# Two transformer layers on one core: the score matmuls of a step in another order, and one bias addition on another engine

## The chip, the cores and the metric

The kernel runs on one core of a Trainium2 chip. A core has a matrix engine (TensorE, "PE" in the profile, with its weight loads shown as "PEld"), a vector engine (VectorE, "DVE"), a scalar engine (ScalarE, "ACT"), a general engine (GpSimd, "POOL") and an engine that mostly starts transfers (SyncE, "SP"). Each runs its own list of instructions in order, and they meet at semaphores. Matmuls write to eight PSUM banks of 128 partitions by 512 fp32 values; VectorE and ScalarE read them.

The metric is the device time of one execution in microseconds. Three executions took 332.4, 333.36 and 334.31 us, so the median before is 333.36 us.

## The reference

Two layers run one after the other over eight batches of 256 tokens of width 128. Each layer is attention with 16 heads of size 8 and a feed-forward part, each followed by a residual sum and a layer norm:

```python
x = L0_attn_x
x = _layernorm(x + _L0_attn_ref(x, ...), axis=-1)     # 16 heads, softmax over 256 keys
x = _layernorm(x + _L0_ffn_ref(x, ...), axis=-1)      # 128 -> 512, butterfly, gelu, butterfly, 512 -> 128
x = _layernorm(x + _L1_attn_ref(x, ...), axis=-1)     # low-rank q and kv, rope, causal softmax
x = _layernorm(x + _L1_ffn_ref(x, ...), axis=-1)      # silu(gate) * up, dequantised weights
```

The attention of layer 0 and the first half of its feed-forward part are

```python
scores = jnp.einsum('bqhd,bkhd->bhqk', q, k) * scale
attn = jax.nn.softmax(scores, axis=-1)
out = jnp.einsum('bhqk,bkhd->bqhd', attn, v)
...
h = jnp.einsum('bsd,dh->bsh', x, W_exp) + b_exp
h = butterfly(h, up_weights, D_HIDDEN)
h = jax.nn.gelu(h + up_bias, approximate=False)
```

The kernel folds `W_exp` and the butterfly into one 128x512 matrix `wup` and one bias `bhid`, so that the way up of layer 0 is a matmul, a bias per row and a gelu.

## The kernel before

**Heads and steps.** Both layers' batches make one list of 16 batches, so 256 heads in all. The program of every engine is one loop, `for g in STEPS`, in steps of four heads (`QUAD`). The softmax needs the maximum of each row of scores before the exponential, so every head's scores are computed twice: first with queries on the partitions, for the maximum ("max" scores, `max_scores`, line 388), and 12 heads later (`LEAD`) with keys on the partitions, for the exponential ("exp" scores, `exp_scores`, line 398). A third matmul subtracts the maximum in PSUM (`less_maximum`, line 407 in layer 0, line 411 in layer 1). VectorE takes the maxima out of the banks (line 824 in layer 0, lines 830 to 832 in layer 1), TensorE turns eight heads' maxima at a time (`turn_maxima`, line 465), ScalarE copies them to `mt` (line 672), and ScalarE applies Exp to each head's bank (line 728).

**Strips.** A head has eight features, and a matmul of its scores uses 32 of the array's 128 rows. Head m stands in strip m mod 4. So heads g, g+1 are in strips 0 and 1, and heads g+2, g+3 in strips 2 and 3; the maxima of step g are for heads g+12 to g+15, in the same order of strips.

**The two halves of a step on TensorE.** Step g first runs `scores((g+14, g+15), (g, g+1), at)` and then `scores((g+12, g+13), (g+2, g+3), at + 4)`. Each call waits for its four banks, and for the keys and the turned maxima that it needs, all at its head; then it issues the two halves of the two maxima and of the two exp scores in turns, so that all four strips have work, and ends with two `less_maximum`.

**Banks.** The eight banks change roles from step to step: the first half of step g uses banks at to at+3, the second half banks at+4 to at+7. After its scores a step runs other work (projections, transposes, products with V, the feed-forward parts), each in a bank claimed from at to at+3 (`claim`). The second half of the next step takes the banks at to at+3 of the step before: its maxima the first two, its exp scores the last two. So it waits until the other work's banks have been read. Layer 0's claims go to banks 0, 2, 3, 1 in order of claim, layer 1's to 2, 3, 0, 1, and those of the step after the gelu's to 0, 1, 2, 3.

**The way up of layer 0.** Two batches make a tile of 512 tokens; there are four tiles. Tile n's four chunks (line 546) run two in step 32n+52 and two in step 32n+56. VectorE reads each chunk's bank, adds the bias and writes `hid0` (line 893, "room_a" in the profile). It does so after the four maxima of its step, and ahead of the residual sum `r_a` (line 915), of the statistics (lines 793 and 796) and of the next step's maxima. ScalarE applies Gelu to all of `hid0` in step 32n+60 (line 763), with a table load before and after it.

## Time and profile before

| | us |
|---|---|
| median of three executions | 333.36 |
| the profiled execution | 331.46 |
| its span (first to last instruction) | 329.7 |
| TensorE busy | 281.9 (85%) |
| VectorE busy | 263.6 (80%) |
| ScalarE busy | 207.4 (63%) |
| GpSimd busy | 205.6 (62%) |

The profiled execution took 331.46 us, 1.76 us more than its span. The span is what the rows further down divide up. "Busy" leaves out waits, branches and the start of transfers. A busy matrix engine is not an engine at its peak, since matmuls overlap and their ends are modelled. In groups of instructions, the name on the left of the arrow is the tile that is written, and the part behind the last bar is the time in which the engine stood idle just before these instructions, with what ended it.

### The profile page before, as it was taken

What the parts mean: (1) busy time and instruction counts of PE and PEld (TensorE: products, weight loads), DVE (VectorE), ACT (ScalarE), POOL (GpSimd) and SP (SyncE); (2) the same over time, 40 slices, a digit from 0 to 9 for tenths busy, and PEclk for the clock granted to TensorE, in tenths of its full rate; (3) what the DMA queues carried; (4) which work ended last, traced back from release to release, by engine and by line L of the source; (5) the groups of instructions that cost most, each with busy time, mean ns of one, the idle gap of its engine ahead of it and who ended that gap; (6) DMA issues with size and microseconds to landing.
All of it is one profiled execution on the core that took longest, in us unless ns stands there. A gap on an engine that the chain in (4) does not pass through costs nothing.

```text
span 329.7 us, 9464 instructions
## 1 busy us (share of the span) xinstructions
PE 281.9 (85%) x3194; PEld 199.3 (60%) x3194; DVE 263.6 (80%) x1007; ACT 207.4 (63%) x428; POOL 205.6 (62%) x326
## 2 busy tenths in 40 slices
PE   7989989997989989888997887988898888898763
PEld 3667555654666446554675456766676666666553
DVE  4897887879588888899679697687899999965565
ACT  2576865776857668496986569666385757536110
POOL 0549994471348447583779785697769756457332
PEclk9999969999899999999999799997799999899978
DMA  6684250303030220404022130403114040000000
GB/s 229 251 248 158 81 195 3 129 0 129 3 112 18 61 101 18 145 8 139 18 64 99 33 130 6 136 23 99 65 27 153 1 146 4 19 2 17 18 16 32
DMA packets 20495, 25.84 MB, mean 78 GB/s; under 512 B 3744, under 2 KB 14304, under 8 KB 20320
## 3 DMA queue, kind: packets, MB, share of 16 engines
q1 hardware_dynamic: 20016, 24.72, 22.4%
q8 instruction: 26, 0.43, 0.6%
q10 hardware_dynamic: 432, 0.53, 0.5%
q14 instruction: 21, 0.17, 0.2%
HBM read 6.36 MB, written 1.05 MB: 22 GB/s over the span
## 4 chain that ended last, share of the span: by engine, by line
PE 42%; DVE 32%; issue 12%; ACT 7%; POOL 4%; DMA 1%; POOLq 0%; ACTq 0%; DVEq 0%
PE bank L600 13%; DVE mx L824 7%; DVE room_c L832 6%; PE bank L615 4%; PE bank L398 4%; PE bank L388 4%; ACT E L728 3%; PE bank L465 3%; DVE turned L923 2%; PE bank L482 2%; DVE room_a L893 2%; DVE room_c L858 2%; PE bank L556 2%; PE bank L567 2%; DVE mx L832 2%
## 5 line engine op out<-in xcount | busy, mean ns | idle before, releaser
L728 ACT ACTIVATE E<-bank 128x512 f32<-128x512 f32 (+1 forms) x256 | 120.3, 550 | 78.4 <-PE bank L411 41.5
L824 DVE TENSOR_REDUCE mx<-bank 128x2 f32<-128x512 f32 x128 | 78.9, 679 | 9.3 <-PE bank L388 9.2
L832 DVE CUSTOM_DVE_ANT_0 room_c<-bank,mask_sb 128x256 f32<-128x256 f32 (+1 forms) x256 | 72.7, 349 | 1.3 <-PE bank L388 1.1
L398 PE MATMUL bank<-QK 32*128 32x256 f32 x480 | 55.8, 316 | 18.5 <-DVE hid L860 6.8
L388 PE MATMUL bank<-QK 32*128 32x256 f32 x480 | 56.8, 313 | 8.1 <-DVE mx L832 2.6
L600 PE MATMUL bank<-E,V 128*32 128x256 f32 (+1 forms) x1024 | 60.7, 383 | 0.1
L398 PEld LDWEIGHTS bank<-QK 32*128 32x128 f32 x480 | 36.9, 188 | 29.3 <-issue 21.8
L388 PEld LDWEIGHTS bank<-QK 32*128 32x128 f32 x480 | 37.2, 187 | 23.3 <-issue 8.9
L1052 POOL TENSOR_SCALAR_AFFINE_SELECT E<-E 128x512 f32<-128x512 f32 x64 | 39.2, 638 | 11.4 <-ACT E L728 11.3
L600 PEld LDWEIGHTS bank<-E,V 128*32 128x32 f32 x1024 | 31.5, 117 | 23.5 <-issue 7.0
L923 DVE STREAM_TRANSPOSE turned<-bank 128x256 f32<-128x256 f32 x32 | 14.3, 446 | 21.8 <-PE bank L600 21.8
L1059 POOL TENSOR_TENSOR at<-turned,rec 128x256 f32<-128x256 f32 x16 | 10.1, 632 | 28.0 <-DVE rec L945 28.0
L407 PE MATMUL bank<-mt,const_r 32*128 32x512 f32 x128 | 27.6, 419 | 0.0
L1032 POOL TENSOR_TENSOR parts<-qk,parts 128x512 f32<-128x512 f32 x15 | 19.2, 1278 | 13.3 <-ACT parts L698 13.3
L556 PE MATMUL bank<-xt,wf 128*128 128x256 f32 x96 | 25.6, 410 | 1.3 <-ACT E L728 0.9
L411 PE MATMUL bank<-mt,const_r 32*128 32x256 f32 (+1 forms) x256 | 24.5, 275 | 0.0
L990 POOL TENSOR_SCALAR nm_a<-mv_a 128x2 f32<-128x2 f32 x15 | 2.9, 193 | 33.1 <-DVE mv_a L796 33.1
L556 PEld LDWEIGHTS bank<-xt,wf 128*128 128x128 f32 x96 | 18.4, 202 | 4.8 <-ACT E L728 1.5
L832 DVE DVE_READ_ACCUMULATOR2_ANT mx<- 128x1 f32 x256 | 21.2, 83 | 0.0
L411 PEld LDWEIGHTS bank<-mt,const_r 32*128 32x128 f32 x256 | 19.2, 189 | 0.0
L465 PE MATMUL bank<-const_r,mxp 128*128 128x128 f32 x64 | 14.8, 314 | 4.6 <-DVE mx L824 3.5
L735 ACT ACTIVATE QK<-spread_qk 128x1024 fp32r<-128x1024 f32 x16 | 17.2, 1076 | 0.0
(127 smaller groups left out, 558.7 us busy)
## 6 DMA issues: line engine op xcount, KB each, us to landing
spread_qk<-parts SPq DMA_DIRECT2D x30, 256.0 KB, 2.5
spread_qk<-parts SPq DMA_DIRECT2D x60, 128.0 KB, 2.1
room_c<-room_c SPq DMA_DIRECT2D x64, 32.0 KB, 1.9
xb<-x_nat SPq DMA_DIRECT2D x1, 1024.0 KB, 6.9
out<-ln_g SPq DMA_DIRECT2D x7, 128.0 KB, 1.9
xt<-x_t SPq DMA_DIRECT2D x1, 768.0 KB, 6.7
wi<-wi_all SPq DMA_DIRECT2D x1, 576.0 KB, 4.4
room_c<-fac_u SPq DMA_DIRECT2D x1, 508.0 KB, 6.5
```

Of the source, the lines that this page charges most:

```text
L388: ins = nc.tensor.matmul(g_bank["max", m][:, cols], both[:, 0, c * P:(c + 1) * P], both[:, 1, keys], start=True, stop=True)
L398: nc.tensor.matmul(g_bank["exp", m][:, c * T:(c + 1) * T - q0], both[:, 1, c * P:(c + 1) * P], both[:, 0, q0:T], start=(c == 0), stop=False)
L407: ins = nc.tensor.matmul(g_bank["exp", m][:, :].rearrange("p (c t) -> p c t", c=2), ones, most.unsqueeze(1).broadcast_to([STRIP, 2, T]), s ...
L411: ins = nc.tensor.matmul(g_bank["exp", m][:, c * T:(c + 1) * T - c * P], ones, most[:, c * P:T], start=False, stop=(c == 1))
L465: ins = nc.tensor.matmul(bank[:, q * P:(q + 1) * P], mxp[:, n % 2, q, :], const_r[:, 0, :], start=True, stop=True)
L556: ins = nc.tensor.matmul(bank[:, s * T:(s + 1) * T], wf[:, s, c * P:(c + 1) * P], xt[:, i * T:(i + 1) * T], start=True, stop=True)
L600: ins = nc.tensor.matmul(bank[VCOL * j:VCOL * (j + 1), q0:T], values, E[:, (2 * n + e) % E_RING, j, k * T:(k + 1) * T - q0], start=(e == 0 ...
L728: act.activation(E[:, a % E_RING, j, 0:n], g_bank["exp", m][:, 0:n], ACT.Exp, scale=SCALE)\
L824: ins = nc.vector.tensor_reduce(mx[:, n % 2, :, i], bank[:, :].rearrange("p (q k) -> p q k", q=QT), AX.X, ALU.max, negate=True)
L832: ins = nc.vector.tensor_tensor_reduce(out=masked_s[:, at % 2, lo:hi], in0=bank[:, lo:hi], in1=mask_sb[:, T + lo - hi:T], scale=-1.0, scal ...
L923: nc.vector.transpose(turned[:, t, :], g_bank["pv", n][:, 0:T]).then_inc(A["turned"], 1)
L1052: nc.gpsimd.affine_select(out=e, in_=e, pattern=[[0, 4], [1, P]], compare_op=ALU.is_ge, fill=0.0, base=0, channel_multiplier=-1).then_inc( ...
```

## The change

There are two parts.

**The order of the scores.** The function `scores` is split up. In a step, the maxima of heads g+14, g+15 and the exp scores of heads g, g+1 still go in turns, and wait for their four banks first. The wait for the turned maxima (`mt_ready`, in every second step) now stands behind these scores, right ahead of `less_maximum`. Then the exp scores of heads g+2, g+3 wait for their own two banks only, run without maxima between them, and are followed by their `less_maximum`. Then the maxima of heads g+12, g+13 wait for their two banks and run last.

**The bias of the way up.** The read of the chunk's bank with the bias goes from VectorE's list to ScalarE's: an `Identity` with `bias=bhid[:, c:c + 1]`, behind the step's four Exps, its copies of maxima, projection and transposed tokens, and ahead of `high_parts`, `copy_values` and the Gelu.

```diff
-            def scores(maxima, exps, at):
-                for i, m in enumerate(maxima):
-                    take((at + i) % BANKS, ("max", m), A["max_done"], order_of(m))
-                for i, m in enumerate(exps):
-                    take((at + len(maxima) + i) % BANKS, ("exp", m), A["exp_done"], m + 1)
...
+            def step_scores(g, at):
+                ahead = range(g + LEAD, g + LEAD + QUAD)
+                banks_for_maxima(ahead[2:], at)
+                banks_for_exps((g, g + 1), at + 2)
                 for long in range(2):
-                    for m in exps if first else ():
+                    for m in ahead[2:]:
+                        max_scores(m, 1 - long)
+                    for m in (g, g + 1):
                         exp_scores(m, long)
-                    for m in maxima:
-                        max_scores(m, 1 - long)
-                    for m in () if first else exps:
+                if g % 8 == 0:
+                    pe.wait_ge(A["mt_ready"], g // 8 + 1)
+                for m in (g, g + 1):
+                    less_maximum(m)
+                banks_for_exps((g + 2, g + 3), at + QUAD + 2)
+                for c in range(2):
+                    for m in (g + 2, g + 3):
+                        exp_scores(m, c)
+                for m in (g + 2, g + 3):
+                    less_maximum(m)
+                banks_for_maxima(ahead[:2], at + QUAD)
+                for c in (1, 0):
+                    for m in ahead[:2]:
+                        max_scores(m, c)
...
         @block.scalar
...
+                for c in range(HC):
+                    if (n := tile_at(g, AT_UP0[c])) is not None:
...
+                        act.wait_ge(F0["up_ps"], HC * n + c + 1)
+                        act.activation(hid0[:, c, :], g_bank["up0", n, c][:, :], ACT.Identity, bias=bhid[:, c:c + 1]).then_inc(F0["pre_ready"], 1)
...
         @block.vector
...
-                for c in range(HC):
-                    if (n := tile_at(g, AT_UP0[c])) is not None:
...
-                        dve.wait_ge(F0["up_ps"], HC * n + c + 1)
-                        nc.vector.tensor_scalar(hid0[:, c, :], g_bank["up0", n, c][:, :], bhid[:, c:c + 1], None, ALU.add)\
-                            .then_inc(F0["pre_ready"], 1)
```

TensorE's list in one step in the middle of layer 0, behind the first chunks of a tile's way down, before the change. Line 388 is max scores, 398 exp scores, 407 the subtraction of the maximum, 465 the turning of the maxima:

```order
L388 MATMUL bank<-QK 128x256 [waits a_exp_done,a_qk_ready,a_max_done]
L388 MATMUL bank<-QK 128x256
L398 MATMUL bank<-QK 128x256 x2
L388 MATMUL bank<-QK 128x256 x2
L398 MATMUL bank<-QK 128x256 x2
L407 MATMUL bank<-mt,const_r 128x512 x2
L398 MATMUL bank<-QK 128x256 [waits a_exp_done,f0_res_done,a_turned]
L398 MATMUL bank<-QK 128x256
L388 MATMUL bank<-QK 128x256 x2
L398 MATMUL bank<-QK 128x256 x2
L388 MATMUL bank<-QK 128x256 x2
L407 MATMUL bank<-mt,const_r 128x512 x2
```

The same step in the changed program:

```order
L388 MATMUL bank<-QK 128x256 [waits a_exp_done,a_qk_ready,a_max_done]
L388 MATMUL bank<-QK 128x256
L398 MATMUL bank<-QK 128x256 x2
L388 MATMUL bank<-QK 128x256 x2
L398 MATMUL bank<-QK 128x256 x2
L407 MATMUL bank<-mt,const_r 128x512 x2
L398 MATMUL bank<-QK 128x256 [waits a_exp_done]
L398 MATMUL bank<-QK 128x256 x3
L407 MATMUL bank<-mt,const_r 128x512 x2
L388 MATMUL bank<-QK 128x256 [waits f0_res_done,a_turned]
L388 MATMUL bank<-QK 128x256 x3
```

The first six rows are the same. In the second half the wait is split in two, and the four max scores went from between the exp scores to behind the subtraction. In a step whose number is a multiple of eight, the first 407 also has a wait of its own, for `a_mt_ready`, that stood at the head before.

ScalarE's list around the first tile's way up, before (728 is Exp, 672 the copy of the maxima, 682 the copy of a projection, 698 `high_parts`, 707 the copy of V, 763 Gelu):

```order
L728 ACTIVATE E<-bank 128x512 [waits a_pv_ps,a_st_ps] x4
L672 ACTIVATE mt<-bank 128x256 [waits a_st_ps,a_mt_ps]
L682 ACTIVATE qk<-bank,bqk_sb 128x256 [waits a_low_ready,a_qk_ps]
L682 ACTIVATE qk<-bank,bqk_sb 128x256
L698 ACTIVATE parts<-qk 128x512 [waits a_qk_ready,a_qk_out]
L728 ACTIVATE E<-bank 128x512 [waits a_pv_ps,a_st_ps] x8
L672 ACTIVATE mt<-bank 128x256 [waits a_st_ps,a_mt_ps]
```

The same place in the changed program, where every line number is 32 higher and line 786 is the new read with the bias:

```order
L760 ACTIVATE E<-bank 128x512 [waits a_pv_ps,a_st_ps] x4
L704 ACTIVATE mt<-bank 128x256 [waits a_st_ps,a_mt_ps]
L714 ACTIVATE qk<-bank,bqk_sb 128x256 [waits a_low_ready,a_qk_ps]
L714 ACTIVATE qk<-bank,bqk_sb 128x256
L786 ACTIVATE room_a<-bank,bhid 128x512 [waits f0_up_ps,bhid_ready]
L786 ACTIVATE room_a<-bank,bhid 128x512 [waits f0_up_ps]
L730 ACTIVATE parts<-qk 128x512 [waits a_qk_ready,a_qk_out]
L760 ACTIVATE E<-bank 128x512 [waits a_pv_ps,a_st_ps] x4
L786 ACTIVATE room_a<-bank,bhid 128x512 [waits f0_up_ps] x2
L760 ACTIVATE E<-bank 128x512 [waits a_pv_ps,a_st_ps] x4
L704 ACTIVATE mt<-bank 128x256 [waits a_st_ps,a_mt_ps]
```

Two reads stand ahead of `high_parts` in the first of the tile's two steps, and two behind the Exps in the second. On VectorE the four instructions of line 893 are gone, and the transposition of `att` (line 938) and the residual sum (line 915) follow the maxima directly. No transfer is added, removed or moved.

## Rows read from the trace of the kernel before

**Rows 1.** Page, part 1: busy time, share of the span, instructions

```profile
PE 281.9 (85%) x3194; PEld 199.3 (60%) x3194; DVE 263.6 (80%) x1007; ACT 207.4 (63%) x428; POOL 205.6 (62%) x326
```

**Rows 2.** Page, part 4: the chain that ended last, by engine, by line

```profile
PE 42%; DVE 32%; issue 12%; ACT 7%; POOL 4%; DMA 1%; POOLq 0%; ACTq 0%; DVEq 0%
PE bank L600 13%; DVE mx L824 7%; DVE room_c L832 6%; PE bank L615 4%; PE bank L398 4%; PE bank L388 4%; ACT E L728 3%; PE bank L465 3%; DVE turned L923 2%; PE bank L482 2%; DVE room_a L893 2%; DVE room_c L858 2%; PE bank L556 2%; PE bank L567 2%; DVE mx L832 2%
```

**Rows 3.** Stretches of 20 us: busy PE, PEld, DVE, ACT, POOL; PE clock; DMA

```profile
60.00:80.00 20.00, 18.41 (x189) 10.90 (x188) 17.72 (x39) 13.97 (x31) 7.78 (x11) 1.00 0.27 96
...
260.00:280.00 20.00, 16.94 (x250) 13.39 (x254) 19.25 (x110) 13.27 (x30) 12.63 (x26) 1.00 0.18 62
```

**Rows 4.** Page, part 2: TensorE's granted clock in 40 slices, tenths of full speed

```profile
PEclk9999969999899999999999799997799999899978
```

**Rows 5.** Instruction groups: busy us, mean ns, idle before and its releasers

```profile
L728 ACT ACTIVATE E<-bank 128x512 f32<-128x512 f32 (+1 forms) x256 | 120.3, 550 | 78.4 <-PE bank L411 41.5 <-PE bank L407 36.2
...
L398 PE MATMUL bank<-QK 32*128 32x256 f32 x480 | 55.8, 316 | 18.5 <-DVE hid L860 6.8 <-DVE r_a L915 2.8 <-DVE r_g L904 2.5
...
L893 DVE TENSOR_SCALAR room_a<-bank,bhid 128x512 f32<-128x512 f32 x16 | 11.5, 745 | 2.8 <-PE bank L546 2.7
...
L746 ACT ACTIVATE xt<-bank 128x512 f32<-128x512 f32 x4 | 2.5, 618 | 0.0
```

**Rows 6.** Chain, first tile, steps 56 and 60: start us, length us, what

```profile
76.16 1.88 DVE mx L824 x3
...
78.38 1.39 DVE room_a L893 x2
...
81.53 0.69 PE bank L465 x2
```

**Rows 7.** Timeline, first tile: start us, length us, engine, what [idle before]

```profile
78.11 0.61 PE L578 MATMUL bank<-wproj_sb,att 128*128 128x128 f32 x4
...
79.69 0.41 DVE L915 TENSOR_TENSOR r_a<-bank,xb 128x256 f32<-128x256 f32 x1
...
80.25 0.38 PE L398 MATMUL bank<-QK 32*128 32x256 f32 x2 [0.85 <-DVE r_a L915]
```

**Rows 8.** Timeline, second tile, steps 88 and 92

```profile
116.48 0.61 PE L578 MATMUL bank<-wproj_sb,att 128*128 128x128 f32 x4
...
118.05 0.41 DVE L915 TENSOR_TENSOR r_a<-bank,xb 128x256 f32<-128x256 f32 x1
```

**Rows 9.** Timeline, third tile, steps 116 to 124

```profile
149.94 0.39 ACT L672 ACTIVATE mt<-bank 128x256 fp32r<-128x256 f32 x1
151.24 2.07 ACT L728 ACTIVATE E<-bank 128x512 f32<-128x512 f32 x4 [0.92 <-PE bank L407]
...
153.83 0.61 PE L578 MATMUL bank<-wproj_sb,att 128*128 128x128 f32 x4
...
155.28 0.41 DVE L915 TENSOR_TENSOR r_a<-bank,xb 128x256 f32<-128x256 f32 x1
```

**Rows 10.** Timeline, fourth tile, steps 152 and 156

```profile
190.00 1.64 ACT L728 ACTIVATE E<-bank 128x384 f32<-128x384 f32 x4 [3.49 <-PE bank L411]
...
192.40 0.61 PE L490 MATMUL bank<-wl,xt 128*128 128x128 f32 x4
...
194.88 0.38 PE L398 MATMUL bank<-QK 32*128 32x256 f32 x2 [1.26 <-DVE room_a L893]
```

**Rows 11.** Timeline, step 200: a second half with its banks already free

```profile
246.71 0.30 PEld L411 LDWEIGHTS bank<-mt,const_r 32*128 32x128 f32 x4
...
246.84 0.39 PE L398 MATMUL bank<-QK 32*128 32x256 f32 x2
```

**Rows 12.** Timeline, step 56: a second half behind its wait

```profile
75.41 0.39 PE L398 MATMUL bank<-QK 32*128 32x256 f32 x2 [0.22 <-issue]
...
75.72 0.41 PE L407 MATMUL bank<-mt,const_r 32*128 32x512 f32 x2
```

**Rows 13.** Waits: who waited for whom: us in total, times, longest

```profile
PE bank L388 <- ACT mt L672: 1.7, 4, 0.6
```

More of the change, by code:

```diff
@@ L413, in less_maximum, with banks_for_maxima @@
                 ins.then_inc(A["st_ps"], 1)
-            def scores(maxima, exps, at):
-                for i, m in enumerate(maxima):
-                    take((at + i) % BANKS, ("max", m), A["max_done"], order_of(m))
-                for i, m in enumerate(exps):
-                    take((at + len(maxima) + i) % BANKS, ("exp", m), A["exp_done"], m + 1)
+            def banks_for_maxima(maxima, i):
+                for m in maxima:
+                    take(i % BANKS, ("max", m), A["max_done"], order_of(m))
+                    i += 1
                 for m in maxima:
@@ L428, in scores, with banks_for_exps, maxima_at_first, last_scores @@
                         pe.wait_ge(A["qk_ready"], 2 * (b - 1) + m % H // 8 + 1)
+            def banks_for_exps(exps, i):
                 for m in exps:
-                    if m % 8 == 0:
-                        pe.wait_ge(A["mt_ready"], m // 8 + 1)
-                first = exps and exps[0] % QUAD == 2
+                    take(i % BANKS, ("exp", m), A["exp_done"], m + 1)
+                    i += 1
+            def maxima_at_first(maxima, at):
+                banks_for_maxima(maxima, at)
+                for c in (1, 0):
+                    for m in maxima:
+                        max_scores(m, c)
[3 more added lines that the diff above has]
+                banks_for_exps((g, g + 1), at + 2)
                 for long in range(2):
-                    for m in exps if first else ():
+                    for m in ahead[2:]:
+                        max_scores(m, 1 - long)
+                    for m in (g, g + 1):
                         exp_scores(m, long)
-                    for m in maxima:
-                        max_scores(m, 1 - long)
-                    for m in () if first else exps:
+                if g % 8 == 0:
[9 more added lines that the diff above has]
+                banks_for_maxima(ahead[:2], at + QUAD)
+                for c in (1, 0):
+                    for m in ahead[:2]:
+                        max_scores(m, c)
+            def last_scores(g):
+                banks_for_exps(range(g, g + QUAD), 0)
+                if g % 8 == 0:
+                    pe.wait_ge(A["mt_ready"], g // 8 + 1)
+                for long in range(2):
+                    for m in range(g, g + QUAD):
                         exp_scores(m, long)
-                for m in exps:
+                for m in range(g, g + QUAD):
                     less_maximum(m)
@@ L500, in _ @@
             project(1, take(6, ("qk", 1), A["qk_out"], 2))
-            scores((2, 3), (), 0)
-            scores((0, 1), (), 2)
+            maxima_at_first((2, 3), 0)
+            maxima_at_first((0, 1), 2)
             project_group(1, 7)
             project_group(2, 0)
-            scores((6, 7), (), 4)
-            scores((4, 5), (), 6)
+            maxima_at_first((6, 7), 4)
+            maxima_at_first((4, 5), 6)
             project_group(3, 1)
             project_values(0, take(3, ("v", 0), A["v_ready"], 1))
-            scores((10, 11), (), 4)
-            scores((8, 9), (), 6)
+            maxima_at_first((10, 11), 4)
+            maxima_at_first((8, 9), 6)
             turn_maxima(0, take(2, ("mt", 0), A["mt_ready"], 1))
@@ L516, in _ @@
                 if g + LEAD < HEADS:
-                    scores((g + LEAD + 2, g + LEAD + 3), (g, g + 1), at)
-                    scores((g + LEAD, g + LEAD + 1), (g + 2, g + 3), at + QUAD)
+                    step_scores(g, at)
                 elif g < HEADS:
-                    scores((), range(g, g + QUAD), 0)
+                    last_scores(g)
                 if (n := half_at(g, AT_MT)):
```

8 lines of the change are left out of this document (4 added, 4 removed).

## The prediction

> **What bounds the kernel now.** I read the busy shares first. TensorE is busy 85% of the span, VectorE 80%, ScalarE 63% [rows 1]. No engine is full, so the order of the work counts. The chain that ended last says whose work it is: 42% TensorE, 32% VectorE, 12% issue and only 7% ScalarE [rows 2]. The chain goes to and fro between TensorE and VectorE; ScalarE is seldom on it. By stretches, VectorE is busy 17.7 of 20 us at 60 to 80 us and 19.3 of 20 us at 260 to 280 us, beside 18.4 and 16.9 us of TensorE [rows 3]. So a VectorE instruction less shortens the run where it stands in the chain, and one more on ScalarE is cheap where that engine idles: it idles 78.4 us just ahead of Exps alone [rows 5]. The read with the bias (line 893) is named in the chain with 2%, about 6.6 of 329.7 us [rows 2].
>
> **The bias on ScalarE.** Removed from VectorE: 16 instructions of 745 ns, 11.9 us by the mean, 11.5 us without overlaps [rows 5]. Added to ScalarE: 16 of about 618 ns, the nearest row being its copy of a bank of the same shape [rows 5], 9.9 us. What that saves is read tile by tile from what becomes late next.
>
> The Trainium skill speaks against this move: "ScalarE: Activation LUTs", section "Rules for kernel authors", gives additions to VectorE, and puts an ACTIVATE at some 0.3 us plus 0.83 ns per element, 0.725 us for 512 as an estimate. By that price the 16 would be 11.6 us, not 9.9, still inside ScalarE's idle time. The trace has the copy at 618 ns against VectorE's 745 ns [rows 5], so here ScalarE isn't the slower of the two.
>
> First tile. The chain runs through VectorE alone from 76.16 us: maxima, two reads of line 893 (78.38, 1.39 us), the residual sum, statistics, then a maximum that releases the turning of the maxima at 81.53 us [rows 6]. Without line 893 the residual sum is next held by its projection on TensorE, 78.11 + 0.61 = 78.72 us. It started at 79.69 [rows 7]. With 0.05 us for the signal that is 0.92 us earlier, and everything behind it moves along: TensorE's second half of scores waited 0.85 us for just this sum [rows 7]. ScalarE's two copies come behind its four Exps; the last of those ends at about 78.3 us when the first pair of this tile has delayed them by one us, and 78.3 + 1.2 = 79.5 is still ahead of 80.25, when that half started.
>
> Second tile. The projection ends at 116.48 + 0.61 = 117.09 us, the sum started at 118.05 [rows 8]: 0.91 us.
>
> Third tile. The projection ends at 154.44, the sum started at 155.28 [rows 9]: 0.79 us. But here ScalarE is late with the first pair. Its copy of the maxima ends at 150.33, two copies more end at 151.55, and the Exps started at 151.24 [rows 9], so this step's scores come about 0.3 us later. I take 0.5 us.
>
> Fourth tile. TensorE's second half of step 156 waited 1.26 us for line 893 and started at 194.88 us [rows 10]. ScalarE's Exps end at 191.64, its copies could end at about 193.2, and the first half starts at 193.01, when the V projection is done [rows 10]; so the second half could start at about 193.4. ScalarE's copy of V is 0.2 us later in exchange. I take 1.3 us of the 1.5.
>
> Sum: 0.92 + 0.91 + 0.5 + 1.3 = 3.6 us. Bounds: nothing (each gain is lost in a later wait) and 6.6 us (all that the chain gives to line 893).
>
> **The order of the scores.** The number of matmuls is the same. There are 61 steps with both kinds. Three effects:
>
> (a) The maxima of heads g+12, g+13 come last. In a half as it is, the subtraction starts 0.31 us after the first exp scores [rows 12]; each strip needs this time whether or not the other two strips work. So the exp scores don't get faster, and the maxima run beside the subtraction. A weight load behind satisfied waits starts in such a place: in step 200 the subtraction's loads start at 246.71 and the next half's, on the other strips, at 246.84 us, 0.13 us later [rows 11]. TensorE's half then ends about 0.13 us later, in the steps whose exp banks are the last to come free. These are about half the steps as an estimate: lines 860, 904 and 915 are what the exp scores mostly waited for [rows 5], and layer 1's first claims are exp banks. 31 x 0.13 = 4.0 us of TensorE's time, at its 42% of the chain 1.7 us. VectorE doesn't see the delay: it is at the first pair of maxima (76.16: three take 1.88 us, two 1.25 [rows 6]) when the second pair gets ready.
>
> (b) Where the maxima's banks are the late ones, exp scores and subtraction run during the wait. That saves up to 0.35 us each, but mostly the wait is hardly longer than the first half itself, so I count some three places, 0.6 us.
>
> (c) The wait for `mt` goes behind four pairs of scores: at most the 1.7 us that line 388 waited for it [rows 13], and I take 0.5, since the subtraction still waits.
>
> Net: 1.7 - 0.6 - 0.5 = 0.6 us slower, of which I take 0.4, since VectorE hides part of (a) at 260 to 280 us [rows 3]. Bounds: 2.5 us faster (all of b and c, none of a) and, from the first rival below, 10 us slower.
>
> **The sum.** 3.6 - 0.4 = 3.2 us less. The profiled execution would take 331.46 - 3.2 = 328.3 us. It lies 1.9 us under the median of the runs shown, so against that median I say 333.36 - 3.2 = **330.2 us**.
>
> **Rivals.**
>
> *Slower: every wait inside a step empties the array.* The new order puts one more waiting weight load into each of 61 steps, on other strips than those that work. If such a load starts only when the subtraction is over, 76.13 in the case of [rows 12], the two pairs of max scores add their own 0.31 us and a start-up of 0.1 us, 0.4 us per step: 24 us of TensorE's time, by its 42% of the chain 10 us on the path. Less 3.6 us that is 6.6 us slower, 340.0 us; it decides from 0.15 us on the path per step on. For it: most second halves in the trace start only behind the subtraction's columns. Against it: they had real waits there, and step 200 shows the overlap with satisfied ones [rows 11]. 13%. The Trainium skill, "TensorE: Matmul & The Clock Gate", section "The mechanism" (of packing small matmuls), has weight loads overlap running matmuls only where the row groups differ. Here they differ, so by that rule this rival is out; the one row agrees, but it can't tell how often.
>
> *No change: the gain is taken by the next in line.* ScalarE's list is strict, and its copies stand behind four Exps and ahead of `high_parts`. If all four tiles go like the third, 0.5 us each, 2.0 us is left; with (a) at 1.7 and nothing from (b) and (c), 0.3 us: 333.1 us. For it: in layer 1 VectorE is full [rows 3], and what TensorE gains there is given back. Against it: three of the four tiles have ScalarE idle where the copies go. 25%.
>
> *More than forecast.* The chain gives line 893 6.6 us, and the scores' order may give 2.5 us: up to 9 us, 324.3 us. TensorE's clock can help or harm in any case: it is granted in full (2.4 GHz) in most slices, with a few at 7 or 8 tenths [rows 4], that is a part of the slice at 1.2 GHz. Such a slice of 8.2 us loses 1.6 to 2.5 us of TensorE's work, and which waits bring one about changes with every shift. 4% for more than 7 us; the clock is why my range is wide.
>
> **The numbers.** Forecast as such (2 to 7 us faster): 57%. A measurement of this kernel can tell about 0.5%, 1.7 us, from no change. Faster by more than that: the forecast and the third rival, 0.61. Within it: 0.25, nearly all from the second rival. Slower: the first rival and a bad turn of the clock, 0.14. The range of 8 in 10 is 325.5 to 335.5 us: it takes in the forecast, the second rival and the mild end of the first.
>
> **What the profile after should show.** No line 893 on VectorE; 16 reads of `room_a<-bank,bhid` on ScalarE with a mean of 0.6 to 0.7 us and hardly any idle time of TensorE that ends with them. The residual sum of steps 56, 88, 120 within 0.1 us of its projection's end. VectorE's busy time 252 us. In a step with free banks, max scores that start within 0.15 us of the subtraction's loads; if instead they start 0.3 us behind it in most steps, the first rival is right. The mean of VectorE's wait for line 388 ahead of maxima should not grow. I am wrong on the mechanism if the wait of ScalarE's Exps grows by more than the 3 us at the tiles, or if the time before the first tile's way up (72 us) has moved by more than 1 us either way: that part has only the new order in it.

## The result and the profile after

The changed kernel takes 327.19 us (median of 20 executions, 324.24 to 330.09), the kernel before 331.86 us (median of 20, 328.09 to 336.25). The ratio is 0.9889, with a 95% interval of 0.986 to 0.9918: 3.7 us faster by the ratio, 4.7 us by the medians. The two differ since ratios, here and further down, leave out executions that are more than 1.5% above the fastest of their kernel, and medians keep them. The forecast was 330.2 us, 3.2 us faster. The profiled execution took 324.52 us, its span is 322.8 us. It is 6.9 us faster than the profiled one of before (331.46 us), so these two traces differ by more than the kernels do on the whole.

The page of the changed kernel: busy shares, then the chain by engine and by line, as in [rows 1, 2].

```profile
PE 278.5 (86%) x3194; PEld 198.7 (62%) x3194; DVE 252.5 (78%) x991; ACT 215.7 (67%) x444; POOL 205.4 (64%) x326
...
PE 52%; DVE 26%; issue 11%; ACT 8%; POOL 1%; POOLq 0%; ACTq 0%; DVEq 0%
PE bank L632 15%; DVE mx L864 6%; PE bank L388 5%; ACT E L760 4%; PE bank L647 4%; PE bank L578 4%; DVE room_c L872 4%; PE bank L398 4%; PE bank L498 3%; PE bank L515 3%; DVE room_c L898 2%; DVE turned L954 2%; PE bank L588 2%; PE bank L599 2%; PE bank L610 2%
```

VectorE lost 11.1 us of work and fell from 32 to 26% of the chain; TensorE rose from 42 to 52%, ScalarE only from 7 to 8%. The bias is no longer among the fifteen lines that the page names: two of the new reads are on the chain, at 109.56 and 146.24 us, 1.4 us together, where about 6.6 us of line 893 were.

Groups of the changed kernel, as in [rows 5] (busy, mean ns, idle time just before and what ended it):

```profile
L760 ACT ACTIVATE E<-bank 128x512 f32<-128x512 f32 (+1 forms) x256 | 119.6, 551 | 65.4 <-PE bank L411 39.1
L864 DVE TENSOR_REDUCE mx<-bank 128x2 f32<-128x512 f32 x128 | 79.3, 681 | 11.2 <-PE bank L388 11.2
...
L388 PE MATMUL bank<-QK 32*128 32x256 f32 x480 | 56.8, 311 | 7.7 <-DVE mx L872 3.1
L398 PE MATMUL bank<-QK 32*128 32x256 f32 x480 | 51.9, 312 | 12.1 <-DVE hid L900 7.0
...
L786 ACT ACTIVATE room_a<-bank,bhid 128x512 f32<-128x512 f32 x16 | 10.7, 705 | 0.7 <-PE bank L578 0.5
```

The idle time ahead of exp scores went from 18.5 to 12.1 us, that ahead of Exp from 78.4 to 65.4 us. The new read on ScalarE takes 705 ns, where the nearest row had 618.

The first tile in the changed kernel, as in [rows 7] (start, length, engine, what, idle before):

```profile
77.41 1.32 ACT L786 ACTIVATE room_a<-bank,bhid 128x512 f32<-128x512 f32 x2
77.50 0.61 PE L610 MATMUL bank<-wproj_sb,att 128*128 128x128 f32 x4
...
78.14 0.42 DVE L946 TENSOR_TENSOR r_a<-bank,xb 128x256 f32<-128x256 f32 x1 [0.68 <-PE bank L610]
...
78.78 0.39 PE L398 MATMUL bank<-QK 32*128 32x256 f32 x2
```

The projection (line 610) ends at 78.11 and the residual sum (line 946) starts at 78.14: VectorE, which was late, now waits. The second half of scores starts 1.28 us behind the projection's start, before it was 80.25 - 78.11 = 2.14 us [rows 7]: 0.86 us gained, where 0.92 was forecast. What releases that half now is ScalarE's read, whose pair ends at 78.73:

```profile
78.78 0.18 PEld L398 LDWEIGHTS bank<-QK 32*128 32x128 f32 x2 [0.32 <-ACT room_a L786]
```

In the second tile the sum follows its projection in the same way, 0.03 us behind the end at 112.88 + 0.61 = 113.49 us:

```profile
112.88 0.61 PE L610 MATMUL bank<-wproj_sb,att 128*128 128x128 f32 x4
...
113.52 0.42 DVE L946 TENSOR_TENSOR r_a<-bank,xb 128x256 f32<-128x256 f32 x1 [0.58 <-PE bank L610]
```

The third tile, as in [rows 9], in the same columns:

```profile
145.40 0.39 ACT L704 ACTIVATE mt<-bank 128x256 fp32r<-128x256 f32 x1
145.67 1.28 ACT L786 ACTIVATE room_a<-bank,bhid 128x512 f32<-128x512 f32 x2
...
147.09 0.39 PE L398 MATMUL bank<-QK 32*128 32x256 f32 x2 [0.67 <-ACT room_a L786]
...
149.56 0.61 PE L610 MATMUL bank<-wproj_sb,att 128*128 128x128 f32 x4
...
150.21 0.42 DVE L946 TENSOR_TENSOR r_a<-bank,xb 128x256 f32<-128x256 f32 x1 [0.68 <-PE bank L610]
...
150.78 0.38 PE L398 MATMUL bank<-QK 32*128 32x256 f32 x2
```

Here the cost that the prediction named shows: TensorE's half at 147.09 waits 0.67 us for ScalarE's first pair. The sum again starts 0.04 us behind its projection.

The fourth tile, as in [rows 10]:

```profile
185.94 0.61 PE L523 MATMUL bank<-wl,xt 128*128 128x128 f32 x4
...
186.97 0.38 PE L398 MATMUL bank<-QK 32*128 32x256 f32 x2
```

From the V projection's start to that half 1.03 us, before 194.88 - 192.40 = 2.48 us: 1.45 gained, where 1.3 was forecast.

Step 200 in the changed kernel, a half with its banks free, as in [rows 11]:

```profile
237.75 0.18 PEld L388 LDWEIGHTS bank<-QK 32*128 32x128 f32 x2
237.81 0.33 PE L388 MATMUL bank<-QK 32*128 32x256 f32 x2
237.83 0.21 PEld L411 LDWEIGHTS bank<-mt,const_r 32*128 32x128 f32 x2
237.86 0.19 PEld L388 LDWEIGHTS bank<-QK 32*128 32x128 f32 x2
237.95 0.25 PE L411 MATMUL bank<-mt,const_r 32*128 32x128 f32 x2
237.98 0.22 PE L388 MATMUL bank<-QK 32*128 32x128 f32 x2
```

The max scores' loads, which have a wait of their own now, start at 237.75 and 237.86 us, around one of the subtraction's at 237.83: in this step the array doesn't drain. The last max scores start 0.03 us behind the last subtraction and end with it, 237.98 + 0.22 = 237.95 + 0.25 = 238.20 us, where the forecast had the half end 0.13 us later. In the third tile, where the exp banks were the late ones, the max scores follow the exp scores within 0.12 us (147.21 behind 147.09) and end before the subtraction does:

```profile
147.21 0.38 PE L388 MATMUL bank<-QK 32*128 32x256 f32 x2
...
147.43 0.38 PE L407 MATMUL bank<-mt,const_r 32*128 32x512 f32 x1
147.44 0.22 PE L388 MATMUL bank<-QK 32*128 32x128 f32 x1
```

The granted clock, as in [rows 4]:

```profile
PEclk9999978999999999999997997999999779899978
```

The mean granted clock is 0.954, before it was 0.955. Where it isn't 2.4 GHz it is 1.2 GHz, so the time at half clock is twice the missing share times the span: 2 x (1 - 0.954) x 322.8 = 29.7 us, and before 2 x (1 - 0.955) x 329.7 = 29.7 us. In these two executions TensorE spent the same time at half clock, at other places.

### The profile page after: what moved, and what is told of

Read it like the earlier page. It is cut to its first block, busy times and chain, and to the rows that moved or that the text cites. A ratio compares the mean times of both kernels' runs of the same rounds, so it can differ in the third digit from the quotient of the medians.

```text
span 322.8 us, 9463 instructions
## 1 busy us (share of the span) xinstructions
PE 278.5 (86%) x3194; PEld 198.7 (62%) x3194; DVE 252.5 (78%) x991; ACT 215.7 (67%) x444; POOL 205.4 (64%) x326
## 4 chain that ended last, share of the span: by engine, by line
PE 52%; DVE 26%; issue 11%; ACT 8%; POOL 1%; POOLq 0%; ACTq 0%; DVEq 0%
PE bank L632 15%; DVE mx L864 6%; PE bank L388 5%; ACT E L760 4%; PE bank L647 4%; PE bank L578 4%; DVE room_c L872 4%; PE bank L398 4%; PE bank L498 3%; PE bank L515 3%; DVE room_c L898 2%; DVE turned L954 2%; PE bank L588 2%; PE bank L599 2%; PE bank L610 2%
## 5 line engine op out<-in xcount | busy, mean ns | idle before, releaser
L760 ACT ACTIVATE E<-bank 128x512 f32<-128x512 f32 (+1 forms) x256 | 119.6, 551 | 65.4 <-PE bank L411 39.1
L864 DVE TENSOR_REDUCE mx<-bank 128x2 f32<-128x512 f32 x128 | 79.3, 681 | 11.2 <-PE bank L388 11.2
L388 PE MATMUL bank<-QK 32*128 32x256 f32 x480 | 56.8, 311 | 7.7 <-DVE mx L872 3.1
L398 PE MATMUL bank<-QK 32*128 32x256 f32 x480 | 51.9, 312 | 12.1 <-DVE hid L900 7.0
L632 PE MATMUL bank<-E,V 128*32 128x256 f32 (+1 forms) x1024 | 62.1, 389 | 0.2
L388 PEld LDWEIGHTS bank<-QK 32*128 32x128 f32 x480 | 38.4, 187 | 23.3 <-issue 9.8
L954 DVE STREAM_TRANSPOSE turned<-bank 128x256 f32<-128x256 f32 x32 | 14.3, 447 | 24.7 <-PE bank L632 24.6
L407 PE MATMUL bank<-mt,const_r 32*128 32x512 f32 x128 | 26.4, 419 | 0.0
L1090 POOL TENSOR_TENSOR at<-turned,rec 128x256 f32<-128x256 f32 x16 | 10.1, 631 | 25.2 <-DVE rec L976 25.2
L411 PE MATMUL bank<-mt,const_r 32*128 32x256 f32 (+1 forms) x256 | 22.3, 276 | 0.0
L1021 POOL TENSOR_SCALAR nm_a<-mv_a 128x2 f32<-128x2 f32 x15 | 2.9, 194 | 29.3 <-DVE mv_a L836 29.3
L411 PEld LDWEIGHTS bank<-mt,const_r 32*128 32x128 f32 x256 | 18.1, 190 | 0.0
L498 PEld LDWEIGHTS bank<-const_r,mxp 128*128 128x128 f32 x64 | 10.1, 199 | 12.9 <-DVE mx L864 9.4
```

Source lines behind the costliest of these rows:

```text
L388: ins = nc.tensor.matmul(g_bank["max", m][:, cols], both[:, 0, c * P:(c + 1) * P], both[:, 1, keys], start=True, stop=True)
L398: nc.tensor.matmul(g_bank["exp", m][:, c * T:(c + 1) * T - q0], both[:, 1, c * P:(c + 1) * P], both[:, 0, q0:T], start=(c == 0), stop=False)
L407: ins = nc.tensor.matmul(g_bank["exp", m][:, :].rearrange("p (c t) -> p c t", c=2), ones, most.unsqueeze(1).broadcast_to([STRIP, 2, T]), s ...
L411: ins = nc.tensor.matmul(g_bank["exp", m][:, c * T:(c + 1) * T - c * P], ones, most[:, c * P:T], start=False, stop=(c == 1))
L498: ins = nc.tensor.matmul(bank[:, q * P:(q + 1) * P], mxp[:, n % 2, q, :], const_r[:, 0, :], start=True, stop=True)
L632: ins = nc.tensor.matmul(bank[VCOL * j:VCOL * (j + 1), q0:T], values, E[:, (2 * n + e) % E_RING, j, k * T:(k + 1) * T - q0], start=(e == 0 ...
```

## The experiments

Every execution comes with its mean granted clock, from which its time at half clock follows as above. Within one kernel it spreads by some 5 us (one standard deviation), and over the 220 executions of the table, each taken against the mean of its own row, a microsecond more of it goes with 0.36 us more of time (correlation 0.90). The last two columns use this and rest on all executions: the mean half-clock time, and the mean time less 0.36 us for each microsecond at half clock beyond 35, with two standard errors. I call it the evened time. It was worked out after the runs, from all executions; the expectations don't know it, but for the last.

A correlation doesn't say what causes what. In one place the traces show the direction: of before and e6, which both have the bias on VectorE, only before has a half-clock stretch at 81 us, and between the ends of the Exps of steps 60 and 72 it takes 1.6 us longer than e6. How the order of the work brings such stretches about, no run here shows. The mean half-clock time of a kernel is itself uncertain, by two standard errors of 1 to 4 us, and 6 us for e6.

| kernel | median us | ratio, 95% interval | at half clock, us | evened time, us |
|---|---|---|---|---|
| before (86 executions of four jobs) | 331.99 | 1 | 33.5 | 332.7 ± 0.2 |
| changed (first comparison) | 327.19 | 0.9889 [0.986, 0.9918] | 34.4 | 327.6 ± 0.3 |
| e1 bias alone | 327.57 | 0.9871 [0.9831, 0.991] | 33.9 | 328.1 ± 0.4 |
| e2 order alone | 330.51 | 0.9955 [0.9919, 0.9991] | 32.4 | 332.2 ± 0.4 |
| e3 `mt` wait alone | 331.54 | 0.9992 [0.9957, 1.0026] | 33.5 | 332.2 ± 0.5 |
| e4 changed, again | 328.14 | 0.9825 [0.9781, 0.9869] | 34.6 | 327.8 ± 0.8 |
| e5 order with one wait | 332.47 | 1.0012 [0.998, 1.0045] | 32.6 | 333.1 ± 0.4 |
| e6 order, maxima first | 328.69 | 0.9887 [0.984, 0.9935] | 25.2 | 332.9 ± 0.5 |
| e7 changed, claims 0, 1, 2, 3 | 338.0 | 1.0183 [1.0135, 1.023] | 40.9 | 336.2 ± 0.3 |
| e8 changed, third tile's pair on VectorE | 326.96 | 0.9843 [0.979, 0.9896] | 33.3 | 327.4 ± 0.7 |
| e9 changed, maxima first | 327.02 | 0.9866 [0.9821, 0.991] | 29.3 | 329.0 ± 0.7 |
| e10 the same in layer 1 alone | 327.12 | 0.9853 [0.9801, 0.9906] | 33.3 | 327.9 ± 1.0 |
| e11 changed, max scores doubled | 331.48 | 1.0006 [0.9964, 1.0048] | 38.2 | 330.0 ± 0.4 |
| e12 order, maxima first in layer 1 | 329.37 | 0.9909 [0.9871, 0.9948] | 28.2 | 332.2 ± 0.6 |

### The parts by themselves

e1: the kernel before with the bias on ScalarE only. e2: the changed kernel with the bias back on VectorE.

```diff
# e1, against before
+                        act.activation(hid0[:, c, :], g_bank["up0", n, c][:, :], ACT.Identity, bias=bhid[:, c:c + 1]).then_inc(F0["pre_ready"], 1)
...
-                        nc.vector.tensor_scalar(hid0[:, c, :], g_bank["up0", n, c][:, :], bhid[:, c:c + 1], None, ALU.add)\
-                            .then_inc(F0["pre_ready"], 1)
```

> The order of the scores as before, only the read with the bias on ScalarE. Theory of the prediction: nearly the whole gain is here, 3.6 us of 3.2 net, so a ratio to before of about 0.989, with the residual sums of steps 56, 88 and 120 right behind their projections. Rival (the order carries a good part of the gain): ratio 0.992 to 0.996, the rest being in the other kernel of this set.

> Only the new order of the scores, the read with the bias stays on VectorE. Theory of the prediction: 0.4 us slower, ratio 1.001 (0.996 to 1.003). Rival, drawn from the trace of the changed kernel, where the second pair's subtraction ends 0.22 us behind the first pair's in place of 0.65 us in steps whose maxima banks are late: some 24 such steps with 0.25 us of TensorE's time each, 6 us, by its 42% of the chain 2.5 us, ratio 0.992 to 0.994. If a waiting load emptied the array: 1.02 or more.

The bias alone gives 0.9871, 4.3 us, as the prediction's theory had it (0.989) and not the rival's (0.992 or more). The order alone gives 0.9955, 1.5 us, between the forecast's range (0.996 and up) and the rival's (0.994 and down); its interval touches both. The product is 0.9827, and the changed kernel in the same job (e4) gave 0.9825. At equal half-clock time the bias is worth 4.6 ± 0.5 us and the order 0.5 ± 0.5 us, 5.1 together, where the changed kernel has 5.1 ± 0.4 in the first comparison and 4.9 ± 0.8 in e4. So the two parts add up, as far as this noise lets one tell.

e3 is the kernel before with nothing moved but the wait for the turned maxima:

```diff
                 for m in exps:
-                    if m % 8 == 0:
-                        pe.wait_ge(A["mt_ready"], m // 8 + 1)
...
+                for m in exps:
+                    if m % 8 == 0:
+                        pe.wait_ge(A["mt_ready"], m // 8 + 1)
                 for m in exps:
                     less_maximum(m)
```

> The kernel before with nothing changed but the wait for the turned maxima, which goes from the head of the half to right ahead of the subtraction. Theory of the prediction: 0.5 us faster, ratio 0.9985, hard to tell from 1. Rival: it carries most of what the new order gives, ratio 0.993; then the first steps' gain of 0.5 us in the changed kernel's trace (ahead of step 4) shows here alone and more comes in layer 1.

0.9992, with an interval from 0.9957 to 1.0026: it can't be told from nothing. Evened it is 0.5 ± 0.5 us.

e4 is the changed kernel as it is.

> The changed kernel as it is, on the same chip as the other three, so that the parts can be added up. Both theories: ratio 0.986 to 0.992. If bias only and order only add up to it, the two parts are independent; if it is less than their sum, one part takes the waits of the other.

Its 0.9825 lies below the range that both theories gave (0.986 to 0.992), and its interval, up to 0.9869, hardly overlaps with that of the first comparison, from 0.986, though the kernel is the same. A ratio from one job can be off by as much as the order is worth. At equal half-clock time the two agree: 327.8 ± 0.8 and 327.6 ± 0.3 us.

### The split wait against the place of the subtraction

e5 keeps the new order but waits for all four banks at the head of the second half, as before:

```diff
                 for m in (g, g + 1):
                     less_maximum(m)
+                banks_for_maxima(ahead[:2], at + QUAD)
                 banks_for_exps((g + 2, g + 3), at + QUAD + 2)
...
-                banks_for_maxima(ahead[:2], at + QUAD)
```

> Only the new order of the scores (the bias stays on VectorE), but the second half of a step waits for all four of its banks, and for the turned maxima's keys, at its head, as before; the two max scores still run last. Order alone measured 0.9955 of the kernel before. Theory A, the split wait: the gain is that the exp scores no longer wait for the two banks of the maxima, and with one wait it is gone: 1.000 to 1.004, the maxima's place behind the subtraction costing up to 0.13 us in the steps with free banks. Theory B, the place of the subtraction: with exp scores and subtraction ahead of the four max scores, Exp of heads g+2, g+3 can start some 0.4 us earlier in each step, whatever the wait: 0.994 to 0.997, as the order alone.

1.0012 against 0.9955, as theory A had it (1.000 to 1.004), and evened 0.9 us slower than e2 (two standard errors: 0.6). What little the order gives comes from the split wait; with one wait the new order is 0.4 ± 0.5 us slower than before. The list of waits has a trace of it: stalls of TensorE's exp loads that the profile puts down to no other engine ("issue"), with their time, number and longest. The row of the kernel before:

```profile
PEld bank L398 <- issue: 21.8, 35, 1.5
```

of e5, order with one wait:

```profile
PEld bank L398 <- issue: 21.8, 34, 1.5
```

of e2, with the split wait:

```profile
PEld bank L398 <- issue: 4.8, 12, 1.0
```

of the changed kernel:

```profile
PEld bank L398 <- issue: 5.0, 13, 1.0
```

and of e6, further down:

```profile
PEld bank L398 <- issue: 2.3, 4, 0.9
```

35 such stalls before, 34 with the new order and one wait, 12 and 13 with the split wait. Most of this time reappears under other names: all idle time ahead of the exp loads is 28.6 us in e5 and 23.3 in e2, that ahead of the exp matmuls 17.9 and 15.1 us. Nor are these stalls a price: e6 has 4 of them and 13.5 us of idle time ahead of its exp loads, and at equal half-clock time it is no faster than before.

e6 turns the second half round: max scores and their wait first.

```diff
                 banks_for_exps((g + 2, g + 3), at + QUAD + 2)
...
-                banks_for_maxima(ahead[:2], at + QUAD)
-                for c in (1, 0):
-                    for m in ahead[:2]:
-                        max_scores(m, c)
# and the same four lines ahead of banks_for_exps
```

> The new order of the scores alone (bias on VectorE), with the second half turned round: max scores of heads g+12, g+13 with their own wait first, then exp scores and subtraction with their own wait. Theory A, the split wait: the exp scores now wait for the maxima's banks again and for the maxima themselves, so the gain is gone and four matmuls (0.3 us on two strips alone) stand ahead: 1.003 to 1.015 of before. Theory B, the place of the subtraction: the same direction, 1.003 to 1.015, since the subtraction is as late as before or later. Theory C, the gain comes from VectorE not being handed maxima of two pairs at once, or from the half-clock stretches alone: 0.995 to 1.000.

All three theories missed: 0.9887, as fast as the whole change. Evened, though, it is 332.9 ± 0.5, no better than before (332.7). TensorE spends 8.3 us less at half clock, which at 0.36 is 3.0 us. With 0.30 or 0.42 in its place e6 comes to 332.3 or 333.5 us, beside 332.6 or 332.8. So by this reckoning the whole gain goes with the clock. It is a reckoning, from six executions; no run held the clock equal. In the stretch from 220 to 300 us (busy PE, PEld, DVE, ACT, POOL; clock; DMA) the kernel before had

```profile
220.00:300.00 80.00, 68.65 (x880) 53.28 (x881) 69.09 (x375) 51.15 (x120) 55.34 (x98) 0.94 0.17 55
```

and e6

```profile
220.00:300.00 80.00, 71.14 (x915) 57.17 (x914) 71.96 (x386) 53.56 (x125) 57.15 (x101) 0.98 0.17 55
```

35 more matmuls in the same 80 us, at a clock of 0.98 in place of 0.94. The profiled execution of e2, with 335.54 us the longest of its twelve, had 0.87 there, with 861 matmuls.

### Banks, the third tile

e7 gives layer 1's claims the order 0, 1, 2, 3, in the changed kernel:

```diff
-                    i = ((0, 2, 3, 1) if g < NB * H else (2, 3, 0, 1))[i]
+                    i = ((0, 2, 3, 1) if g < NB * H else (0, 1, 2, 3))[i]
```

> The changed kernel with layer 1's claims in the order 0, 1, 2, 3 in place of 2, 3, 0, 1. The work claimed first in a step is read first, so its banks become those of the next step's max scores, and the work claimed last (a gate that VectorE reads last) those of the exp scores. For the changed kernel the new split wait favours late banks under the maxima. If the last claims of a step are what its exp scores wait for under 0, 1, 2, 3, this is slower, 1.005 to 1.015 of the changed kernel, by the split wait; if most steps of layer 1 have four claims with the slow reads among the first two, it is faster, 0.985 to 0.995. Against the kernel before: 0.97 to 1.00. If the split wait is worth nothing, it equals the changed kernel, 0.983 to 0.989 of before.

338.0 us, 1.0183, slower than the changed kernel by 3.3%. Every expectation missed: 0.97 to 1.00 of before, and 0.5 to 1.5% at most against the changed kernel. The direction is the one given for exp scores that wait for the last claims, but that isn't what the trace shows. Its groups:

```profile
L388 PE MATMUL bank<-QK 32*128 32x256 f32 x480 | 58.0, 316 | 11.1 <-DVE hid L900 4.4
...
L398 PE MATMUL bank<-QK 32*128 32x256 f32 x480 | 54.6, 320 | 3.2 <-ACT room_a L786 0.9
```

The late gates (line 900) are now waited for by the max scores, 11.1 us against 7.7, and exp scores wait 3.2 us against 12.1. The waits went to where the split wait was meant to help, and the time rose. The edit moves the banks of all of layer 1's other work too, so it doesn't price the split wait; it shows that late banks on that side are no gain in themselves. The list of waits shows where the time appears: VectorE's wait for the products with V, 24.6 us in the changed kernel, here

```profile
DVE turned L954 <- PE bank L632: 35.8, 24, 3.6
```

These products stand behind the late maxima in TensorE's list. Whether that makes up the rest of the loss wasn't tried; 6.5 us more at half clock are 2.3 us of it, and 8.6 us evened remain.

e8 leaves the first two chunks of the third tile on VectorE:

```diff
-                    if (n := tile_at(g, AT_UP0[c])) is not None:
+                    if (n := tile_at(g, AT_UP0[c])) is not None and not (n == 2 and c < 2):
...
+                        nc.vector.tensor_scalar(hid0[:, c, :], g_bank["up0", n, c][:, :], bhid[:, c:c + 1], None, ALU.add)\
+                            .then_inc(F0["pre_ready"], 1)
```

> The changed kernel with the first two chunks of the third tile's way up read by VectorE, as before; the other 14 stay on ScalarE. The prediction held that in the third tile ScalarE is late with its first pair and that only 0.5 us of that tile's 0.9 is gained. If so, this kernel is 0.0 to 0.5 us faster than the changed one at that step, and if VectorE is what the step waits for, 0.5 us slower; in the median no difference that can be told, 0.983 to 0.989 of before. The step-end times of the trace around 155 us tell it: later than the changed kernel's by 0.5 to 1 us if VectorE sets them.

The timeline of e8 at the place of the third tile:

```profile
144.75 1.47 DVE L933 TENSOR_SCALAR room_a<-bank,bhid 128x512 f32<-128x512 f32 x2
145.08 0.39 ACT L704 ACTIVATE mt<-bank 128x256 fp32r<-128x256 f32 x1
...
146.37 0.38 PE L398 MATMUL bank<-QK 32*128 32x256 f32 x2 [0.26 <-DVE room_a L933]
```

From the copy of the maxima to that half it is 1.29 us here and 1.69 us in the changed kernel: ScalarE's lateness with the first pair costs 0.4 us there, within the 0.0 to 0.5 expected. The median, 326.96 us, can't tell it.

### Does maxima first add to the change, and what holds the clock

e9 is the changed kernel with e6's second half; e10 has it only from step 128 on.

```diff
# e10, against the changed kernel; e9 without the two conditions
+                if g >= NB * H:
+                    banks_for_maxima(ahead[:2], at + QUAD)
+                    for c in (1, 0):
+                        for m in ahead[:2]:
+                            max_scores(m, c)
                 banks_for_exps((g + 2, g + 3), at + QUAD + 2)
...
+                if g < NB * H:
```

> The changed kernel (bias on ScalarE) with the second half of a step turned round: max scores of heads g+12, g+13 behind their own wait first, then exp scores and subtraction behind theirs. With the bias on VectorE this order measured 0.9887 of before, against 0.9955 for the changed kernel's order, and the bias alone 0.9871. If the two add up: 0.9887 x 0.9871 = 0.976 of before, some 324 us, with at most 7 stretches of TensorE at half clock. Rival, the gain of this order came by chance from where the half-clock stretches fell in that job: 0.983 to 0.990 of before, as the changed kernel, with 8 to 10 such stretches.

> The changed kernel with maxima first only from step 128 on (layer 1's heads), and the changed kernel's order in layer 0. If what maxima first brings is brought in layer 1, by VectorE getting its next maxima earlier and TensorE's half-clock stretches between 220 and 300 us going (three in the changed kernel, none in the trace with maxima first), and costs some 0.5 to 1 us in layer 0: 0.972 to 0.978 of before, and no half-clock stretch or one from 220 to 300 us. Rival, it is brought in layer 0 or nowhere: 0.980 to 0.990.

0.9866 and 0.9853: both as the changed kernel, and the gain of e6 does not add to that of the bias. The two rivals that said so were right on the time. The reason given for e9, that e6's clock had been chance, isn't borne out: in another job e9 has 29.3 us at half clock, 5.1 less than the changed kernel, with two standard errors of 2.9. Evened, e9 is 1.4 ± 0.8 us slower than the changed kernel; the two nearly cancel.

e11 issues max scores again in layer 1, to see whether more work holds the clock:

```diff
-                for c in (1, 0):
+                for c in (1,) if g < NB * H else (1, 1, 1):
                     for m in ahead[:2]:
                         max_scores(m, c)
+                for m in ahead[:2]:
+                    max_scores(m, 0)
```

> The changed kernel, with the second half's four long max scores and two more issued again behind the first ones in layer 1 (the halves of 256 keys three times in place of once, the same values each time): 116 more matmuls, some 0.2 us of TensorE in each of 29 steps, 6 us in all, on work that changes nothing. Theory of the clock: TensorE is granted half its clock in layer 1 where it is the least busy, so the added work keeps it up; the half-clock stretches between 190 and 300 us (four in the changed kernel) fall to two or fewer, which gives back about 1.7 us each; with 42 to 50% of 6 us on the path the time is 0.980 to 0.990 of before, near the changed kernel's. Rival, the stretches don't depend on how busy TensorE is: as many as before and the added work on top, 0.990 to 1.003.

1.0006, in the rival's range (0.990 to 1.003) and outside the theory's (0.980 to 0.990). The stretch from 190 to 300 us, first of the changed kernel, then of e11:

```profile
190.00:300.00 110.00, 93.77 (x1237) 73.20 (x1226) 90.57 (x487) 69.46 (x156) 77.11 (x136) 0.94 0.16 52
```

```profile
190.00:300.00 110.00, 96.25 (x1250) 76.80 (x1247) 88.91 (x486) 69.32 (x154) 74.37 (x126) 0.91 0.17 55
```

The time at half clock in this stretch rose from 2 x 0.06 x 110 = 13 us to 2 x 0.09 x 110 = 20 us. TensorE is busier, but matmuls at half clock are also busy for longer (four of line 523 in e6 took 0.66 us at 83.46 us, at a clock of 1.00, and 1.17 us at 120.51, at 0.50), so the busy time alone says little. Over all executions the half-clock time rose from 34.4 to 38.2 us: more work on TensorE didn't hold the clock. Evened, the added matmuls cost 2.3 ± 0.5 us, some 39% of the 6 us estimated for them; the chain had given TensorE 42% before and 52% after.

e12 is e2 with maxima first from step 128 on.

> The bias stays on VectorE; the scores' order is the changed kernel's up to step 124 and maxima first from step 128 on. Over all runs so far, within a kernel each microsecond that TensorE spends at half clock goes with 0.36 us of time. Maxima first in both layers had 25 us at half clock against 33.6 of before, and 0.9887. Theory 1, the clock in layer 1: the steps from 128 on, with maxima first, keep the clock up, and this kernel has 24 to 28 us at half clock and 0.985 to 0.990 of before. Theory 2, the order in layer 0 or its interplay with both: 30 us or more at half clock and 0.993 to 1.000. At equal time at half clock both expect -1.0 to +0.5 us against before.

28.2 ± 2.9 us at half clock and 0.9909: just outside the first theory's numbers and nearer to them than to the second's. Evened it is 0.5 us faster than before, as both expected. Layer 1's steps seem to bring the larger part of the clock's gain while the bias is on VectorE. With the bias on ScalarE (e10) the same steps show none, 33.3 ± 4.0 us; from six executions that is no proof. Why is not settled.

## Why the prediction was right

The sign, the size and the range held, and the larger of the two terms was right step by step. The smaller, the order's, had the wrong sign; that the number didn't suffer is due to its being small. By its own steps:

**The bias: 3.6 us forecast, 4.3 us (1.29%) measured.** The differences of the times at which each step's last Exp ends, before against changed, give 1.0 us for the first tile (steps 52 to 72: 2.6, less 1.6 for a half-clock stretch that only the kernel before has there), 1.2 for the second (84 to 104), 0.5 for the third (112 to 132) and 1.2 for the fourth (152 to 156), 3.9 us; in e1 3.7 us. The 1.6 us are the same that before and e6 differ by over that stretch. Forecast were 0.92, 0.91, 0.5 and 1.3. The rest of the 4.3 is not placed. The method, to ask at each place what is late next once the instruction is gone, gave each tile within 0.3 us. The share of the chain, 6.6 us, was half as much again as the truth.

**ScalarE's price: 618 ns forecast, 705 measured.** It changed little: ahead of the Exps ScalarE's idle time fell by 13.0 us, and of TensorE's idle time only 0.9 us ahead of exp scores ends with a new read. The third tile's 0.4 us, which e8 shows, were in the forecast with 0.3. The Trainium skill's page "ScalarE: Activation LUTs", section "Rules for kernel authors", was nearer with some 0.3 us plus 0.83 ns per element, 0.725 us as an estimate. The same section gives additions to VectorE. This case's measurement goes against that: with 16 of them on ScalarE, which had 7% of the chain where VectorE had 32%, the kernel was 4.3 us faster (e1).

**The order: 0.4 us slower forecast; 1.5 us faster measured, 0.5 ± 0.5 us at equal half-clock time.** This term had the wrong sign. Its true size is nearly in the noise. (a), the late place of the maxima, was forecast at 1.7 us and is e5 less the `mt` wait, 0.4 + 0.5 = 0.9 ± 0.7 us. It was probably too large since in a step with late exp banks the two kinds still run together (the third tile above), and in one with free banks the half ends with its subtraction (step 200), not 0.13 us later. These are single steps; a count over all 61 wasn't made. (b), the split wait, was forecast at 0.6 and is e5 less e2, 0.9 ± 0.6 us; the three places that it was counted at weren't looked for. (c) was forecast at 0.5 and measured at 0.5 ± 0.5 us.

**The rivals.** The emptied array did not come: it would have cost 10 us, and e2 is faster than before; step 200 shows the loads side by side. Its limit of 0.15 us per step is TensorE's time and not the path's: 61 x 0.15 x 0.42 = 3.8 us make up for the bias. The gain taken by the next in line came in the third tile alone, as forecast. "More than forecast", 324.3 us, is as far from the 327.19 as the forecast is, on the other side, but none of its reasons applied: the chain's 6.6 us for line 893 did not come, nor the 2.5 us of the order.

**The baseline.** 330.2 us was set against 333.36, the median of three; over 86 executions the kernel before has 331.99. Of the 3.0 us between forecast and result 1.4 us are this, and the two terms above make up the other 1.6: 0.7 of the bias (4.3 - 3.6) and 0.9 of the order (0.4 + 0.5). As a ratio the forecast was 0.9904, the result 0.9889.

**The named signs.** VectorE's busy time 252.5 (252 forecast), the sums within 0.04 us of their projections, the reads' mean 0.705 just over the 0.6 to 0.7 given. The mean of VectorE's waits for line 388 ahead of maxima should not grow, and it didn't: 9.2 us in 12 waits ahead of line 824 before, 11.2 us in 16 ahead of the same instruction, now line 864. Their sum did grow, by 2.0 us. The time before the first tile moved by 0.5 us, and that isn't the order's: it is there at the end of step 0, where e2, with the same order, is 1.2 us later than before. ScalarE's idle time ahead of Exps was not to grow by more than 3 us; it fell from 78.4 to 65.4 us.

## What to carry to other kernels

Price the removal of an instruction at the place where it stands, by what is late next there, not by its share of the chain; 3.6 us so found stood against 6.6 by the share and 4.3 measured. Before one explains a difference of 1% by the order of the work, the mean granted clock of all executions has to be laid beside their times: here one order had 1.1% that all went with the clock, and nothing at equal half-clock time. A split wait is no end in itself: where another order of banks put the late ones on the side that it waits for separately, the time rose by 3%.

## What was not expected of the hardware

The read of a PSUM bank with a bias on ScalarE took 705 ns, its copy of a bank of the same shape without one 618 ns [rows 5]. Within a kernel, time at half clock varies from execution to execution, and most of the spread of 2% goes with it: 0.36 us per us, correlation 0.90. With another order and other waits of the same matmuls it went from 33.5 to 25.2 ± 6.0 us (e6), with another order of banks from 34.4 to 40.9 ± 1.7 us (e7), and with 116 more matmuls from 34.4 to 38.2 ± 2.0 us (e11).
